# Power attention and a mixture of experts: the last batch routed in a half and two quarters, and an expert's rows turned ahead of its silu steps

## What is computed

```
x = layernorm(x + attention(x))        # 16 query heads on 8 key heads, a = (q.k*scale)^2 * exp(gate), causal,
                                       # y = a@v / (sum(a) + 1e-6), then y @ Wc + bc
x = layernorm(x + ffn(x))
ffn: scores = softmax(x @ gate_w.T); the best 6 of 64 experts per token, weights normed to sum 1
     every (token, expert) pair gets a slot in its expert's table, in order of the tokens, at most 768
     expert: (silu(rows @ wg.T) * (rows @ wu.T)) @ wd.T, weighted, added up per token
     plus a shared expert of twice the width on every token
```

## Time and profile before

| | |
|---|---|
| median of 3 runs | 2226.1 us (2224.7 to 2226.31) |
| the profiled execution | 2232.49 us |
| its span, first to last instruction | 2230.7 us |
| PE busy | 2137.1 us, 96% |
| DVE, ACT, POOL busy | 1292.4, 1157.8, 756.2 us |
| mean granted clock of TensorE | 0.979 |

### The profile page before, as it was taken

One profiled execution on the slowest core, in us unless ns is written; L12 is line 12 of the kernel. 1 busy time (PEld: TensorE's weight loads), 2 busy tenths in 40 slices (PEclk: granted clock), 3 DMA queues, 4 the chain that ended last, 5 costly groups with the idle time before them and its releaser, 6 DMA issues.

```text
span 2230.7 us, 38654 instructions
## 1 busy us (share of the span) xinstructions
PE 2137.1 (96%) x14567; PEld 1958.3 (88%) x14570; DVE 1292.4 (58%) x2841; ACT 1157.8 (52%) x2201; POOL 756.2 (34%) x752
## 2 busy tenths in 40 slices
PE   8999999999999999999999999999887999999992
PEld 6999998999999899999989899999866889999992
DVE  4444444454565545456564566445763688888875
ACT  4444544454444445444444444445433678778874
POOL 3121112000000551000054102430241578878885
PEclk9999999999999999999999999999988899999996
DMA  4866642112111421311142211322434699999977
GB/s 161 332 273 265 272 160 69 44 55 83 34 60 46 141 94 52 94 36 60 35 152 94 91 53 56 106 77 64 139 137 157 152 233 232 234 224 233 235 140 244
DMA packets 146642, 302.28 MB, mean 136 GB/s; under 512 B 20336, under 2 KB 82544, under 8 KB 146448
## 3 DMA queue, kind: packets, MB, share of 16 engines
q1 hardware_dynamic: 104960, 247.34, 32.6%
q0 software_dynamic: 41056, 51.96, 11.9%
q10 hardware_dynamic: 432, 0.44, 0.1%
HBM read 160.57 MB, written 142.67 MB: 136 GB/s over the span
## 4 chain that ended last, share of the span: by engine, by line
PE 78%; issue 6%; DVE 5%; POOL 5%; DMA 4%; ACT 2%; another core or an unknown queue 0%; POOLq 0%; ACTq 0%; DVEq 0%; SPq 0%
PE bank L1011 47%; PE bank L1443 22%; POOL y_part L2503 5%; PE bank L1020 4%; DMA y_part<-y_e,row_token 3%; PE bank L1456 2%; PE bank L1561 1%; DVE stats L2410 0%; DMA gw_raw<-in_gw 0%; DVE xe_lo L2327 0%; PE bank L1487 0%; ACT silu_b L1795 0%; ACT y_e L1862 0%; DVE bank L2237 0%
## 5 line engine op out<-in xcount | busy, mean ns | idle before, releaser
L1443 PEld LDWEIGHTS bank<-v,a 128*128 128x128 f32 x4608 | 603.3, 191 | 42.8
L1443 PE MATMUL bank<-v,a 128*128 128x129 f32 x4608 | 616.8, 274 | 0.0
L2503 POOL DMA_INDIRECT y_part<-y_e,row_token x234 | 362.6, 1550 | 140.6 <-issue 65.9
L2476 POOL TENSOR_TENSOR decay_all<-decay_all,tab 128x128 f32<-128x128 f32 x128 | 59.4, 464 | 846.5 <-DMA decay_all<-decay_dram 846.2
L1741 ACT ACTIVATE a<-bank,c_s 128x512 f32<-128x512 f32 x384 | 262.9, 686 | 160.6 <-PE bank L1011 144.1
L1745 ACT ACTIVATE a<-ub 128x512 f32<-128x512 f32 (+1 forms) x256 | 133.9, 524 | 353.8 <-DVE ub L2050 328.3
L2493 POOL DMA_INDIRECT slots<-rows,slot_u x192 | 189.6, 988 | 296.1 <-DVE slot_u L2216 126.5
L1011 PE MATMUL bank<-q_hi,k_hi 128*128 128x512 f32 (+1 forms) x640 | 264.1, 413 | 2.7 <-DVE ub L2050 2.7
L1011 PE MATMUL bank<-q_lo,k_hi 128*128 128x512 f32 (+1 forms) x640 | 237.2, 371 | 0.0
L1011 PE MATMUL bank<-q_hi,k_lo 128*128 128x512 f32 (+1 forms) x640 | 236.3, 369 | 0.0
L2029 DVE TENSOR_TENSOR q_lo<-bank,q_hi 128x512 fp32r<-128x512 f32 x128 | 88.4, 690 | 201.3 <-ACT q_hi L1721 191.3
(11 more groups left out here) (247 smaller groups left out, 4758.9 us busy)
## 6 DMA issues: line engine op xcount, KB each, us to landing
slots<-acc SPq DMA_DIRECT2D x64, 816.0 KB, 7.8
w_raw_f<-in_wffn SPq DMA_DIRECT2D x68, 624.0 KB
decay_all<-decay_dram SPq DMA_DIRECT2D x128, 128.0 KB
xr<-slots SPq DMA_DIRECT2D x18, 544.0 KB
xr<-slots SPq DMA_DIRECT2D x20, 476.0 KB
w_hi<-w_dram SPq DMA_DIRECT2D x24, 384.0 KB
w_lo<-w_dram SPq DMA_DIRECT2D x24, 384.0 KB
wc_hi<-wc_dram SPq DMA_DIRECT2D x24, 256.0 KB, 2.8
```

Of the source, the lines that this page charges most:

```text
L1443: ins = e.matmul(dst[:, tt, r, :], a32[u % NA][:, r, t0:t0 + P], v[n % 3][:, s, :], start=(s == 0 and r == 0), stop=(s == 2 * g + tt), ski ...
L2476: e.tensor_tensor(arg[:, GROUP:GROUP + P], arg[:, P:GROUP], mask, ALU.add)
L2503: e.indirect_dma_start(out=y_part[part], out_offset=bass.IndirectOffsetOnAxis(ap=token, axis=0), in_=y_rows, in_offset=None, bounds_check= ...
```

## The change

1. `PARTS` gets a half and two quarters for the last batch: `FIRST_HALF` (tiles 0 to 3), `QUARTER_A` (4, 5) and `QUARTER_B` (6, 7). A part with one pair needs no `again`, as `onehot` still holds it.
2. `LAST_UNITS` takes group 2 of both heads ahead of group 3 of both: the last unit of group 2 is now number 25 instead of 37. `last_at` follows; the mask buffers go by the group's place in the order (`em_at`), not by its number.
3. `route_at` gives each step of the first half a unit (from 17 to 34, `again` and `send` among them) and the first 7 steps of quarter A too (31 to 39); `TOGETHER` is gone.
4. The passage has an order of its own: quarter A's other steps and all of quarter B's among the shared expert's jobs 0 to 4, `rank_keys` behind job 4's gate_up instead of job 6's, `raw_in` of four experts ahead of job 6, the first expert's split behind job 8, `turn(SEQ[0])` ahead of the second expert's split.
5. In the experts' loop `turn` of the next expert stands ahead of `hidden(k, 0)` and `hidden(k, 1)` ahead of both `split_lo`; `hidden(k, 3)` is last; `raw_in` is ahead of `rows_in`, and `load_count` stands between them.
6. Two things that follow: the x1t of the second half no longer uses `yt_hi`/`yt_lo`, and `shared_down` doesn't wait for all of x1t any more. `x_at` shifts the two buffers of the experts' rows.

```diff
+HEAD_A, HEAD_B = LAST, LAST + 1
+LAST_UNITS = (diagonal(HEAD_A, 0) + before(HEAD_A, 1) + before(HEAD_B, 1)[:1] + diagonal(HEAD_A, 1) + before(HEAD_B, 1)[1:]
+              + diagonal(HEAD_B, 0) + diagonal(HEAD_B, 1) + before(HEAD_A, 2) + before(HEAD_B, 2)[:2] + diagonal(HEAD_A, 2)
+              + before(HEAD_B, 2)[2:] + before(HEAD_A, 3)[:2] + diagonal(HEAD_B, 2) + before(HEAD_A, 3)[2:] + before(HEAD_B, 3)
+              + diagonal(HEAD_A, 3) + diagonal(HEAD_B, 3))
...
-PARTS = [(b_, 0, TILES) for b_ in range(B - 1)] + [(B - 1, t_, TILES // 2) for t_ in (0, TILES // 2)]
+PARTS = ([(b_, 0, TILES) for b_ in range(B - 1)] + [(B - 1, 0, TILES // 2)]
+         + [(B - 1, t_, TILES // 4) for t_ in (TILES // 2, TILES * 3 // 4)])
...
-             + [f"{what}{q}" for q in pairs for what in ("again", "send")])
+             + [f"{what}{q}" for q in pairs for what in ("again", "send") if what == "send" or len(pairs) > 1])
...
-    first_half_routed_at = 19
+    route_at = {FIRST_HALF: (17, 18, 18, 20, 20, 20, 23, 25, 25, 26, 26, 27, 27, 28, 29, 29, 30, 30, 31, 31, 31, 31, 32, 32, 33, 33, 34, 34),
+                QUARTER_A: (31, 33, 35, 35, 37, 39, 39)}
...
     catch_up()
+    do("add", L, NG - 1)
     do("shared_in", 2)
     do("gate_up", 0, 0)
-    do("experts_begin")
+    do("experts_begin",)
     send_all()
+    on_spare("turn", L + 1, NG - 1)
+    on_spare("project", L, NG - 1)
     do("gate_up", 0, 1)
...
+    route(QUARTER_B, "std")
+    route(QUARTER_A, "hot0")
+    route(QUARTER_A, "chosen0")
+    do("gate_up", 1, 0)
+    do("gate_up", 1, 1)
+    do("gate_up", 1, 2)
+    do("gated", 0, 2)
+    route(QUARTER_A, "chosen_bf")
+    route(QUARTER_A, "weight0")
+    do("gated", 0, 3)
+    route(QUARTER_A, "weight1")
+    route(QUARTER_A, "count")
+    route(QUARTER_A, "taken")
...
+    do("gate_up", 2, 0)
+    route(QUARTER_A, "slots")
     do("gated", 1, 1)
+    route(QUARTER_A, "send0")
+    route(QUARTER_B, "x1t0")
     do("gate_up", 2, 1)
+    do("gate_up", 2, 2)
...
+    route(QUARTER_B, "logit0")
...
     do("shared_in", 5)
+    route(QUARTER_B, "slots")
+    route(QUARTER_B, "send0")
+    do("rank_keys",)
...
+    on_spare("rank_experts",)
+    do("raw_in", MAINS[0])
+    do("raw_in", MAINS[1])
+    do("raw_in", MAINS[2])
+    do("raw_in", MAINS[3])
+    do("gate_up", 6, 0)
...
     for place, x_id in enumerate(SEQ):
         k = KX + place
         later = W_ORDER[NTH[x_id] + 2:NTH[x_id] + 4] if x_id < E else []
-        if later and later[0] >= 0 and place:
-            do("rows_in", later[0])
+        if len(later) > 1 and place:
+            do("raw_in", later[1])
+        up(k, 0)
         if place == 8:
             on_spare("rank_counts")
             do("load_count",)
-        if len(later) > 1 and place:
-            do("raw_in", later[1])
-
-
-        up(k, 0)
-        hidden(k, 0)
+        if later and later[0] >= 0 and place:
+            do("rows_in", later[0])
         if place + 1 < STEPS:
             turn(SEQ[place + 1])
+        hidden(k, 0)
         if later:
             do("split_hi", later[0])
+        hidden(k, 1)
         up(k, 1)
+        up(k, 2)
         if later:
             do("split_lo", later[0], 0)
-        hidden(k, 1)
-        if later:
             do("split_lo", later[0], 1)
-        up(k, 2)
         hidden(k, 2)
         if place:
             down(SEQ[place - 1], (0,))
-        hidden(k, 3)
         if later:
             do("split_lo", later[0], 2)
         if place:
             down(SEQ[place - 1], (1,))
+        hidden(k, 3)
```

More of the change, by code:

```diff
@@ L410, in schedule @@
     left = [item[1:] for item in late]
-    assert left == [("project", HEADS - 1, NG - 2), ("turn", HEADS - 1, NG - 1), ("project", HEADS - 1, NG - 1)], left
-    assert [name for _, name in background] == ["again1", "send1"], background
+    assert left == [("project", L, NG - 1), ("turn", L + 1, NG - 1), ("project", L + 1, NG - 1)], left
+    assert not background
+    to_route = {p: route_steps(p) for p in (QUARTER_A, QUARTER_B)}
+    del to_route[QUARTER_A][:len(route_at[QUARTER_A])]
     def send_all():
@@ L424, in hidden, with shared_end, gated @@
             do("hidden", k, part)
-    def step(name):
-        route_step(B, name)
-        send_all()
-    def early(name):
-        route_step(B - 1, name)
-        send_all()
+    def shared_end(m):
+        for pair in range(MAIN // GROUP):
+            on_spare("shared_down", m, pair)
+        do("shared_out", m)
+        if m + XE < M1:
+            do("shared_in", m + XE)
+    def gated(k, *parts):
+        for part in parts or range(4):
+            do("gated", k, part)
     def turn(x_id):
@@ L437, in turn, with split @@
         do("pick", x_id)
+    def split(x_id):
+        do("split_hi", x_id)
+        for part in range(3):
+            do("split_lo", x_id, part)
     def down(x_id, pairs):
@@ L444, in schedule @@
     catch_up()
+    do("add", L, NG - 1)
     do("shared_in", 2)
     do("gate_up", 0, 0)
-    do("experts_begin")
+    do("experts_begin",)
     send_all()
+    on_spare("turn", L + 1, NG - 1)
+    on_spare("project", L, NG - 1)
     do("gate_up", 0, 1)
-    on_spare("turn", HEADS - 1, NG - 1)
-    do("turn_lo", HEADS - 1, NG - 1)
+    do("turn_lo", L + 1, NG - 1)
+    route(QUARTER_A, "softmax1")
+    route(QUARTER_A, "max")
+    route(QUARTER_A, "index")
+    on_spare("project", L + 1, NG - 1)
@@ L488, in schedule @@
-    do("shared_in", 4)
-    do("shared_out", 0)
-    early("again1")
-    early("send1")
-    step("softmax1")
-    step("max")
+    do("gated", 2, 0)
+    route(QUARTER_B, "logit0")
     do("gated", 2, 1)
     do("gated", 2, 2)
+    route(QUARTER_B, "softmax0")
+    do("shared_in", 4)
+    route(QUARTER_B, "softmax1")
+    route(QUARTER_B, "max")
+    route(QUARTER_B, "index")
+    on_spare("shared_down", 0, 0)
+    on_spare("shared_down", 0, 1)
+    do("shared_out", 0)
     do("gated", 2, 3)
@@ L499, in schedule @@
     do("gate_up", 3, 2)
+    route(QUARTER_B, "hot0")
+    route(QUARTER_B, "chosen0")
+    route(QUARTER_B, "chosen_bf")
     do("gated", 3, 0)
     do("gate_up", 4, 0)
+    do("gated", 3, 1)
     do("gate_up", 4, 1)
-    do("gate_up", 4, 2)
-    do("gated", 3, 1)
-    step("index")
+    route(QUARTER_B, "weight0")
+    route(QUARTER_B, "weight1")
     do("gated", 3, 2)
     do("gated", 3, 3)
-    step("hot0")
-    step("chosen0")
-    step("hot1")
-    step("chosen1")
+    route(QUARTER_B, "count")
+    route(QUARTER_B, "taken")
+    do("gate_up", 4, 2)
     on_spare("shared_down", 1, 0)
@@ L560, in schedule @@
     on_spare("shared_down", 3, 0)
+    do("gated", 8, 0)
     on_spare("shared_down", 3, 1)
     do("shared_out", 3)
-    do("gate_up", 8, 2)
     do("gate_up", 9, 0)
@@ L610, in schedule @@
     do("counted",)
-    turn(SEQ[0])
     for place, x_id in enumerate(SEQ):
@@ L2137, in route @@
                 elif name == "softmax0":
-                    for k in range(nt // 2 - 2, nt // 2):
+                    for k in range(max(0, nt // 2 - 2), nt // 2):
                         once.wait_ge(*out_of(("route", p, f"logit{k}")))
```

169 lines of the change are left out of this document (67 added, 102 removed).

## The result

The changed kernel takes 2239.27 us (median of 9 runs, 2234.91 to 2244.69), the kernel before 2226.31 us beside it. The ratio is **1.0054, 95% interval 1.0041 to 1.0068**: slower by 13 us between the medians, where 2216 us, 10 us faster, was forecast. The profiled execution took 2239.27 us, its span is 2237.6.

The account below looks back on a forecast made before the run. PE was taken as the bound of the experts' loop, with time to be had in the passage. From 2232.5 us profiled, -0.1 (waits) and -9.7 (stops) gave 2222.7, and 6.4 less unprofiled gave 2216; range 2191 to 2236 us.

Parts of the forecast that it names:

- What bounds the kernel: Experts' loop: PE, busy 200.00 of 200 us, is the bound, and a new order can't make it faster.
- The terms -1.2 and +0.5: Experts' loop start: half the xe_lo wait goes as rows turn earlier, -1.2 us; SP stops at load_count, +0.5.
- The plain sum, -0.1: Terms of attention's tail, the passage and the loop's start added without the stops: -0.1 us.
- Attention's tail: Attention's last units: waits for norm's rows and yt_lo go, -2.9 us; DVE backlog delays last diagonals, +2.0 (0 to +5).
- The passage's waits: Passage: waits at its two ends go, -2.0 us; DVE backlog before gate_up, +2; quarter B's logit waits for x1t_lo, +1.5.
- has less to do than before: 0: Passage: DVE, busy 71.66 of 126 us, gets less work despite the quarters, so their cost is 0.
- Half clock: Passage: PE's work at half clock behind idle stretches costs 11.4 us; 2.0 us was forecast to return with the stops.
- The stops, -9.7: Passage: engine halts without plain cause, 24.3 us, shrink as scatter trains overlap weight loads less; -9.7 us including half clock.
- The fourth rival: Passage: the stops exist only under the profile and plain waits bound unprofiled runs; -6 us, 2220 us, chance 0.10.
- The slower one: From attention's tail on, scatter trains grow together (36, then 12) with longer stops; +7.5 and -0.1, 2234 us, chance 0.22.
- The stops stay: Passage: as many scatters cost as much stop time, only the waits count; -0.1, 2226 us, chance 0.18.
- The signs: Right: passage 113 to 120 us, last scatter near 1655, no PE wait for norm's rows, loop unchanged; wrong: passage over 126.

Follow-up runs that it names:

- pe_light: The kernel before with one of gate_up's three passes left out from the experts' second step on, so less work for PE; 1.0015.
- loop_only: The kernel before with only the experts' loop body changed to the new one; 1.0002.
- Experiments 3 and 4: Changed kernel, quarters kept, first half's again/send and other routing steps put later in several orders; 1.0070, 1.0060, 1.0048, last order 1.0058 with stops, 1.0092 without.
- passage_only: The changed kernel with the old body of the experts' loop, all changes ahead of the loop kept; 1.0055.
- tail_order: The kernel before with only attention's last units in the new order, routing in halves and loop as before; 0.9987, on a chip with stops.
- repaired: The changed kernel with first half's again and send behind attention, its count, taken and slots at unit 33, first expert's turn last ahead of the loop; 1.0060.
- again_late: The changed kernel with the first half's again and send moved from attention's units 33 and 34 to behind quarter A's index; 1.0070.

## Why the prediction was wrong

**What bounds the kernel.** That PE is the bound of the loop and a new order can't make it faster was wrong in its reason. PE busy 200 of 200 was not the bound: in pe_light it was busy 347.7 us of 400 and the kernel was no faster (1.0015), and another order of the same instructions made the first 40 steps 7 us shorter, which POOL took back later. The terms -1.2 and +0.5 for its start came to 0 together (1.0002), within the error; the wait behind the first step's down fell from 2.4 to 1.7 us in loop_only.

**The plain sum, -0.1, was the step that failed most.** Measured on chips without stops: +14.7 us to the first scatter-add, +12 in the median. By its terms:
- *Attention's tail*, -2.9 + 2.0. The two waits went. The backlog was priced at the masks of the last diagonals, and there it costs 1.4 us (`ub`), which fits the +2.0. Not priced were PE's own routing matmuls in DVE's queue: count at unit 31, in the unit of the chosen_bf that it needs, 2.8 us, and quarter A's x1t behind again and send, 3.5 us. "The score runs three units ahead, which hides 5.7 of the 7 us" holds for scores; x1t and count have no such lead. The three waits are 7.7 us, above my upper bound of +5, and with the half clock behind the last of them the last av matmul came 6.7 us later (1597.2 against 1590.5) instead of 0.9 earlier.
- *The passage's waits*, -2.0 + 2.0 + 1.5. x1t_lo came to 1.6, as said; hb and chosen_bf to 1.0 and 1.1. Of the -2.0 the 0.6 for yt_lo came; the wait for xe_lo at the first turn did not go, it rose from 1.4 to 2.8 us, as the turn's xe_lo now stands behind eight DVE steps of two gated jobs.
- *DVE "has less to do than before: 0".* Its work is the same (112.44 and 113.24 us), but I compared sums and not when it is due. In the first 30 us behind attention DVE must make the gated steps that let PE go on, and the quarters put a second whole chain there. Experiments 3 and 4 fit this: whatever was moved, PE waited for DVE at the next step. That it is the reason is argued, as no order with quarters got rid of the waits.
- *Half clock.* It was given back (-2.0) with the stops; in fact new gaps of 1 to 3.5 us each took 6.1 us of PE's time. Here a microsecond of waiting cost about 1.7 (8.6 idle, 14.7 in all).

**The stops, -9.7.** Measured 0, to about 5 us: 1.0054 for the whole change where the stops are, 1.0055 and 1.0002 for its parts where they are not. Their size was right: 24.3 + 11.4 = 35.7 us was the estimate of what they cost, and the chips differ by 31 to 34. What failed is the step that less of a meeting with the weight loads means less stop. Near the loads PE's issue stops did fall, from 11.4 to 3.6 us (forecast 6.5 or so); but the others rose from 12.9 to 21.2, most of it 8.7 us behind yt_lo and 7.0 behind chosen_bf at the first three trains, and the sum stayed (24.3 and 24.8). The fourth rival, that they are the profile's own, is not settled: every execution listed with the runs has a span and a granted clock beside its time, so each was recorded, and that the chips differ says only that the stops are not on every chip. The Trainium skill, "NOTIFIC — the notification-queue block", section 7.1, says that this block, which the prediction took for the recorder of the profiler's events, holds back inside rather than lose a record; no run here shows whether it did.

**The rivals.** The slower one had the right sign and nearly the time (2234), and the wrong mechanism; that was luck. The trains grew together as it says only where there are no stops. In passage_only:

```profile
1588.53 1.63 POOL L2515 DMA_INDIRECT slots<-rows,slot_u  x1 [37.09 <-DVE slot_u L2238]
...
1624.33 1.01 POOL L2515 DMA_INDIRECT slots<-rows,slot_u  x1 [2.77 <-DVE slot_u L2238]
...
1638.55 0.97 POOL L2515 DMA_INDIRECT slots<-rows,slot_u  x1 [0.30 <-issue]
...
1643.71 0.97 POOL L2515 DMA_INDIRECT slots<-rows,slot_u  x1 [4.19 <-issue]
```

That is 36 scatters but for pauses of 1.95 and 2.9 us, then 12, and PE has no stop; with the stops they came as 24, 12 and 12, and PE's stops stayed as long as before. The loss is the same with no scatter at all. "The stops stay" with a plain sum of +12 instead of -0.1 would have been the forecast.

**The signs.** Of those named, the length of the loop held (454.9 us from first to last scatter-add, 454.3 after); each gap ahead of the last diagonals stayed under 5 us. The passage of 113 to 120 us did not come (it took 131, from 1596.8 to the first expert's gate_up at 1728.1, and over 126 was named as wrong), nor did a last scatter near 1655 (it ended at 1681.8), and quarter A's rows made a wait of 3.5 us where none was to be.

**Open.** What stops the engines on some chips and not on others, the recording of the profile among the candidates: on a chip with stops no kernel without scatters ran. In tail_order the stops move with the trains, but the weight loads and the rest of the passage move too, so this does not single out the scatters. And whether some order with quarters costs nothing: five were tried, the changed kernel's among them, and none with its scatters came under 1.0048.

## What to carry to other kernels

Before moving work of a helping engine forward, write down for each stretch not its busy share but what of its list must be done before the bounding engine's next step; a step moved earlier pushes back all that the other engine is about to wait for. Give every matmul that needs another engine's fresh result a unit of cover of its own, and count a short gap of PE with the half clock behind it. And an engine that is 100% busy in the trace is the bound only when a kernel with less work for it is faster: take work away from it before building on it.

## What the runs showed of the hardware

The same kernel takes 2192 us on three chips and 2224 to 2226 us on others, 1.5% more. Nearly all of it lies in a stretch of some 120 us in which PE, DVE, ACT and SP stop for 1 to 12 us each within or just behind a train of scatters, while POOL goes on inside the train at 1.28 us a scatter. On the short chips such trains stop nobody (24 scatters from 1641.9 us in loop_only, 48 in a row from 1602.0 in repaired). A difference of 0.5% can be read on either sort of chip, but not across them.

A gap of PE of 2.75 us (in front of `count`) was followed by the full granted clock in passage_only (1.00 from 1580.4 to 1587 us) and by half of it for a while in again_late (0.61 in the mean from 1580.6 to 1585). So the same gap can cost nothing more or, by an estimate from these numbers (4.4 us at 0.61), some 1.7 us.
